# A recurrent kernel on one core: the Vector engine's cube reads a scaled copy of q from SBUF, and two Vector instructions change places

## The reference

```python
def cell(h, x):                                   # layer 0, GRU
    gi = x @ W_ih + b_ih
    gh = h @ W_hh + b_hh                          # 512 x 1536
    r, z = sigmoid(i_r + h_r), sigmoid(i_z + h_z)
    n = tanh(i_n + r * h_n)
    return (1.0 - z) * n + z * h

def derivative(q, p, drive):                      # layer 1, four times per step (Runge-Kutta)
    i_couple = tanh(q) @ coupling.T               # 512 x 512
    dq = q - q ** 3 / 3.0 - p + drive + i_couple + bias
    dp = EPSILON * (q + ALPHA - BETA * p)
    return dq, dp

x = x + scan(cell, cond, x)
x = x + scan(rk4 of derivative, cond, x)          # DT = 0.01, clip to +-20 after each step
```

## Time and profile before

| | before |
|---|---|
| median of 3 runs | 3523.38 us (3521.14 to 3523.52) |
| profiled execution | 3529.05 us, its span 3527.2 us |
| busy: PE / PE weight loads / DVE / ACT / POOL | 98% / 90% / 80% / 74% / 42% |
| granted TensorE clock, mean | 0.987 |

### The profile page before, as it was taken

How to read it: one execution, slowest core, us unless ns; L and a number is a source line. 1 busy time by engine, 2 the same in 40 slices (tenths; PEclk the granted TensorE clock), 3 DMA queues, 4 the chain that set the end, 5 groups by cost and what they waited for, 6 DMA issues and landing times.

```text
span 3527.2 us, 296053 instructions
## 1 busy us (share of the span) xinstructions
PE 3439.5 (98%) x115469; PEld 3178.9 (90%) x115469; DVE 2816.7 (80%) x20699; ACT 2605.1 (74%) x23713; POOL 1478.5 (42%) x6169
## 2 busy tenths in 40 slices
PE   8989999999999999999999999999999999999978
PEld 4479999999999999999999999999999999999954
DVE  2068888888888888888888888888888888888876
ACT  3257777777777777777777777777777777777752
POOL 0024444444444444444444444444444444444421
PEclk9999999999999999999999999999999999999978
DMA  3000000000000000000000000000000000000001
GB/s 131 24 26 1 1 1 1 1 1 1 1 1 1 1 1 1 1 1 1 1 1 1 1 1 1 1 1 1 1 1 1 1 1 1 1 1 1 1 2 48
DMA packets 9433, 24.29 MB, mean 7 GB/s; under 512 B 556, under 2 KB 600, under 8 KB 8792
## 3 DMA queue, kind: packets, MB, share of 16 engines
q1 hardware_dynamic: 8832, 19.92, 1.6%
q10 hardware_dynamic: 88, 0.02, 0.0%
HBM read 15.75 MB, written 4.19 MB: 6 GB/s over the span
## 4 chain that ended last, share of the span: by engine, by line
PE 85%; DVE 7%; ACT 6%; issue 2%; DMA 0%; ACTq 0%; DVEq 0%; POOL 0%; POOLq 0%
PE psum L1187 46%; PE psum L1144 32%; PE psum L1114 5%; ACT tpart L583 2%; PE psum L1290 1%; ACT tfull L585 1%; DVE psum L895 1%; DVE tpart L852 1%; ACT qterm L558 1%; ACT pterm L554 1%; DVE psum L875 1%; DVE qnext L895 1%; DVE psum L887 0%; ACT qterm L547 0%; DVE wih L981 0%
## 5 line engine op out<-in xcount | busy, mean ns | idle before, releaser
L1187 PE MATMUL psum<-tpart,cpl 128*128 128x32 f16 (+1 forms) x65536 | 1966.8, 176 | 21.1 <-DVE tpart L852 14.5
L1187 PEld LDWEIGHTS psum<-tpart,cpl 128*128 128x128 f16 x65536 | 1781.8, 96 | 113.0 <-DVE tpart L852 22.8
L1144 PE MATMUL psum<-hpart,whh 128*128 128x32 f16 x49152 | 1553.3, 177 | 15.9 <-DVE hpart L828 12.0
L1144 PEld LDWEIGHTS psum<-hpart,whh 128*128 128x128 f16 x49152 | 1374.4, 96 | 38.3 <-DVE hpart L828 14.2
L852 DVE TENSOR_TENSOR tpart<-tfull,tpart 128x8 f16<-128x8 f32 x4096 | 682.1, 167 | 154.0 <-ACT tfull L585 11.4
L895 DVE TENSOR_REDUCE psum<-psum 128x8 f32<-128x24 f32 x3072 | 574.8, 188 | 110.1 <-PE psum L1187 3.7
L583 ACT ACTIVATE tpart<-psum 128x8 f16<-128x8 f32 x3072 | 527.3, 172 | 90.5 <-DVE psum L895 18.4
L585 ACT ACTIVATE tfull<-psum 128x8 f32<-128x8 f32 x3072 | 526.4, 172 | 0.0
L583 ACT ACTIVATE tpart<-qnext 128x8 f16<-128x8 f32 x1024 | 213.5, 208 | 312.4 <-DVE qnext L895 312.4
L505 ACT ACTIVATE rz<-gates 128x16 f32<-128x16 f32 x1024 | 241.1, 235 | 267.5 <-DVE gates L787 267.0
L547 ACT ACTIVATE qterm<-psum 128x16 f32<-128x16 f32 x3072 | 413.6, 202 | 0.0
(11 more groups left out here) (153 smaller groups left out, 4449.8 us busy)
## 6 DMA issues: line engine op xcount, KB each, us to landing
xrow<-in_x_dram SPq DMA_DIRECT2D x4, 1024.0 KB, 11.7
out_dram<-space SPq DMA_DIRECT2D x16, 256.0 KB, 2.0
wih<-in_L_cond_W_ih_dram SPq DMA_DIRECT2D x3, 1024.0 KB, 10.2
space<-in_L_cond_W_hh_dram SPq DMA_DIRECT2D x1, 3072.0 KB, 19.1
space<-in_L_cond_coupling_dram SPq DMA_DIRECT2D x1, 1024.0 KB, 19.3
xrow<-in_cond_dram SPq DMA_DIRECT2D x1, 1024.0 KB, 4.7
wih<-in_L_cond_Wk_dram SPq DMA_DIRECT2D x1, 1024.0 KB, 5.7
wih<-in_L_cond_Wo_dram SPq DMA_DIRECT2D x1, 1024.0 KB, 7.9
```

The lines of the kernel that those rows point to most:

```text
L1144: mm = pe.matmul(gate_out[x][:, :, :, c * B:(c + 1) * B], whh[:, w, k, n * P:(n + 1) * P], copies_in(hpart[:, k, :, :]), start=(c == 0 and ...
L1187: mm = pe.matmul(stage_out[a][:, 0:reps, :, col:col + B], cpl[:, w, k, n * P:(n + 1) * P], copies_in(tpart[:, s % 2, k, :, :])[:, 0:reps, ...
```

## The change

Three edits, all in the step that the engines repeat:

1. ScalarE makes one scaled copy of `qt` (`COPY_OF` says which), then the square, and then the other copies. Before, all copies stood ahead of the square. In stages 1 to 3 `cubic` multiplies by that copy in SBUF in place of `qt` in PSUM, and `base` divides its factor out. As the square no longer tells that the copies are made, `sum_stage(s, 0)` of stages 1 and 2, which overwrites `qt`, waits for `qterm_ready[s]` as well. In `cubic(0)` the wait for `q1_ready` is left out (`linear` ahead of it has the same).
2. In stage 2 `sum_gates(1, gru)` stands between `cubic(2)` and `base(2)` in place of behind `base(2)`.
3. In stage 3 `sum_stage(3, 0)` stands ahead of `new_h_full(1, gru)`.

```diff
+COPY_OF = [2, 3, 3]
...
-            def stage_terms(s):
+            def stage_terms(s, rs):
-                for r in range(s + 1, 4):
+                for r in rs:
                     ins = act.activation(in_halves(qterm[:, s + 1, r, :]), qt, ACT.Copy, scale=STEP[s] * sums_of[r][s + 2])
-                ins.then_inc(qterm_ready[s + 1], 1)
+                    if r == s + 1:
+                        ins.then_inc(qterm_ready[s + 1], 1)
...
                     if s < 3:
-                        stage_terms(s)
+                        stage_terms(s, [COPY_OF[s]])
...
                         act.activation(in_halves(sq[:, s_next, :]), arg, ACT.Square,
                                        scale=k_stage[s]).then_inc(sq_ready[s_next], 1)
+                    if s < 2:
+                        stage_terms(s, [r for r in range(3, s, -1) if r != COPY_OF[s]])
...
                     dve.wait_ge(sq_ready[0], v - 1)
-                    dve.wait_ge(q1_ready, v)
...
                     dve.wait_ge(sq_ready[s], v)
-                    dve.scalar_tensor_tensor(in_halves(cub), in_halves(sq[:, s, :]), LINEAR[s], qt,
+                    dve.scalar_tensor_tensor(cub, sq[:, s, :], LINEAR[s], qterm[:, s, COPY_OF[s - 1], :],
                                              ALU.add, ALU.mult).then_inc(cub_ready, 1)
...
-                    dve.scalar_tensor_tensor(stage_base, in_halves(cub), -STEP[s - 1] / 3, in_halves(sums[:, s - 1, :]),
+                    dve.scalar_tensor_tensor(stage_base, in_halves(cub), -1 / (3 * sums_of[COPY_OF[s - 1]][s + 1]),
+                                             in_halves(sums[:, s - 1, :]),
                                              ALU.mult, ALU.add).then_inc(base_ready, 1)
...
                 if a == 0:
                     dve.wait_ge(base_ready, stage_count(s, v))
+                    if s in (1, 2):
+                        dve.wait_ge(qterm_ready[s], v)
...
                 cubic(2, now)
-                base(2, now)
                 if gated_step:
                     sum_gates(1, gru)
+                base(2, now)
...
                     new_high(1, gru)
+                sum_stage(3, 0, now)
+                if gated_step:
                     new_h_full(1, gru)
-
-                sum_stage(3, 0, now)
```

More of the change, by code:

```diff
@@ L874, in cubic @@
                     dve.wait_ge(sq_ready[s], v)
-                    dve.scalar_tensor_tensor(in_halves(cub), in_halves(sq[:, s, :]), LINEAR[s], qt,
+                    dve.scalar_tensor_tensor(cub, sq[:, s, :], LINEAR[s], qterm[:, s, COPY_OF[s - 1], :],
                                              ALU.add, ALU.mult).then_inc(cub_ready, 1)
+            sums_of = recovery_sums()
             def base(s, v):
```

## The result

The changed kernel takes 3500.01 us, the median of 4 runs (3494.10 to 3502.56), beside 3523.38 before: a ratio of 0.9933, with a 95% interval from 0.9921 to 0.9944. That is 23 us less, where 66 were forecast. The profiled execution took 3494.10 us, with a span of 3492.3 and a clock of 0.990 (0.987 before).

A forecast was written before the change was run, and what follows sets the result against it. TensorE bounds the kernel, with some 0.6 us of gaps between groups a step to win. Edits 1, 2 and 3 give 0.11 + 0.08 - 0.06 = 0.13 us a step, times 510 = 66 us: 3457 us, range 3420 to 3500.

The forecast's parts named there:

- rival (b): Stages 1 and 2: later base eats edit 2, third semaphore costs 0.06 us; 0.03 a step, 3508 us; chance 0.12.
- 0.06 a step, between 0 and 0.10: Stage 3: edit 3 gains nothing, delays `h_low` and stops TensorE in group 7; costs 0.06 us a step.
- in the steps with the loop's branch all 0.10 pass on: Ahead of group 0, branch steps: edit 3's whole 0.10 us stop in group 7 delays group 0.
- some 0.03: Ahead of group 0, steps without the branch: of edit 3's 0.10 us stop only some 0.03 passes on.
- Edits 1 and 2 together, 0.19: Groups 4 to 6: edit 1 gives 0.11 us a step and edit 2 0.08.
- group 4 starts 0.11 earlier: Stage 1: edit 1 lets the row sum start at 1596.65, not 1596.76, and group 4 start 0.11 us earlier.
- from it to group 4 the chain is untouched: Stage 1: from row sum to group 4 (tanh twice, low part) nothing changes, so the 0.11 us arrives whole.
- Edit 2, "0.08": Stage 2: gates ahead of base let group 6 start at 1599.01, not 1599.09: 0.08 us, between 0 and 0.21.
- I let it move by 0.06: Cube of stage 2 in VectorE's queue: with edit 1 it comes 0.06 us earlier, bounds 0 and 0.11.
- The third semaphore, 0.02: Row sum's extra wait: costs between 0 and 0.06 us, taken as 0.02.
- Rival (c): Stage 3: cube from SBUF waits for GpSimd's L418, starting 0.19 us later; 15 us slower, 3539 us; chance 0.07.
- Square before copies, and cube from SBUF: Edit 1: copies behind the square cost ScalarE nothing; cube's SBUF input costed at 0, though the skill gives 0.065 us shorter.

The follow-up runs named there:

- e1: The changed kernel without edit 3 (edits 1 and 2 alone): 3440.18 us, ratio 0.9764 to the kernel before.
- e2: The kernel before with edit 3 alone: 3589.44 us, ratio 1.0187 to the kernel before.
- e10: e1 with `h_low` of half 1 behind the second row sum of stage 3: 3534.49 us, ratio 1.0018 to the kernel before.
- e9: The changed kernel with TensorE's loop branch behind group 5 in place of group 7, still two steps a turn: 3461.27 us, ratio 0.9812 to the kernel before.
- e3: The kernel before with edit 1 alone: 3517.21 us, ratio 0.9984 to the kernel before.
- e4: The kernel before with edit 2 alone: 3459.72 us, ratio 0.9822 to the kernel before.
- e12: e3 (edit 1 alone) with GpSimd's `next_x1` ahead of its sum of stage 1: 3493.77 us, ratio 0.9902 to the kernel before.
- e5: e1 with GpSimd's `next_x1` ahead of its sum of stage 1: 3428.08 us, ratio 0.9717 to the kernel before.
- e11: e1 with `next_x1` first, the cube of stage 3 on PSUM and the branch behind group 5: 3425.19 us, ratio 0.9706 to the kernel before.

## Why the prediction was off, point by point

The direction and the places were right. The forecast was 66 us, 23 came. The 43 us between are two terms. That 3500 lies near the 3508 of rival (b) is chance: nothing of what (b) supposes was seen.

- **Edit 3, "0.06 a step, between 0 and 0.10": 0.117 to 0.13** (e1 and e2). This is 29 us of the 43, and the size lay outside the bounds. The mechanism was right to 0.02: the row sum gained nothing, `h_low` came 0.19 later, the hole was 0.12 against 0.10. The step that failed is "in the steps with the loop's branch all 0.10 pass on". There 0.18 passes on, since the gap at the branch grows from 0.15 to 0.21 as well (e1, e10). In the others "some 0.03" was too low: 0.06 in the means, as group 0 has a hole of 0.04 besides. The prediction took the gap ahead of group 0 for a cushion and never asked whether the branch itself depends on what stands ahead of it. It does, by the sequencer's lead (e10), and behind group 5 the branch costs nothing (e9). What the sequencer does in the 0.35 us of a branch isn't shown.
- **Edits 1 and 2 together, 0.19: 0.163** (e1, 83 us), 14 us of the 43. **Edit 1, "group 4 starts 0.11 earlier"**: it starts 0.12 earlier in the means, but has a hole of 0.04, so 0.08 is left. The step that failed is "from it to group 4 the chain is untouched", which holds for half 0 only: on half 1 `argument` was held by GpSimd, the second row sum came late, and the 13th product with it. **Edit 2, "0.08"**: with edit 1 in place the gaps ahead of groups 5 and 6 fall from 0.239 to 0.159 together, 0.08 as forecast. Taken alone the edits give other shares, 0.011 (e3) and 0.123 (e4), and that is no second error: by the prediction's own working edit 1 moves `h_low`, and so group 5, by only 0.06, and edit 2 without edit 1 gives up to 0.13. Measured, edit 1 gives 0.068 once `argument` isn't held (e12), and "I let it move by 0.06" was nearly 0 with the hold. With `next_x1` first edits 1 and 2 give 100 us, 0.195 a step (e5), about the 0.19 forecast; since `weigh` and `h_low` are held there, that match is in part luck.
- **The third semaphore, 0.02**: nothing in either stage. Rival (b) falls.
- **Rival (c), the cube blocked by GpSimd**: it is held, by 0.05 and not 0.16. I dismissed the hold with the row of L821 inside L420, which starts 0.12 behind GpSimd's instruction. The held ones start from 0.05 before it to 0.12 behind it: `argument` in the changed kernel, the cube, `weigh` in e5, the low part in e5 and e11. In all these traces they end 0.02 to 0.04 behind the end of GpSimd's instruction. So how much one loses depends on how much earlier it would have ended: low parts of e5 that start 0.10 to 0.12 behind the sum take 0.19, those from 0.14 on their usual 0.17, and `argument` of before, 0.10 behind, would have ended behind the sum anyway. L821 is of another kind: it ends well inside L420 and is free in all 391 such meetings. L420 is another operation (TENSOR_SCALAR) than the held ones met (TENSOR_TENSOR). The evidence was of the wrong kind, and the instruction that mattered was another than the rival named.
- **Square before copies, and cube from SBUF**: free cubes take 176 to 180 ns with both inputs in SBUF, as before with one in PSUM (177). The 0.065 us that the Trainium skill's figures (VectorE: DVE Perf Modes, section on the TRN2 errata) would give doesn't appear.

What stays open: that e5 and e11 end near the same time, although e11 has one more hold removed and the branch moved, is read from their traces (the held low parts, the gap ahead of group 4); no run takes GpSimd's sum away from all of VectorE's instructions at once, so what the holds cost in all isn't known. Why L420 holds nothing isn't tested either. Cubes of stages 1 and 2 from PSUM with ScalarE's copies behind the square weren't tried.

## What to carry to other kernels

An instruction moved between a producer and its consumer in an in-order queue is paid where the consumer gates another engine; look up that engine's need to the hundredth before calling the gap behind it a cushion, and see whether a loop branch stands there. A branch wants a place in the loop ahead of which nothing waits late, and behind which TensorE has to wait anyway: moving it was worth 43 us here for no work at all. When an edit brings one engine forward against another, list which of its instructions will now start together with the other engine's; the swap of two lines in e4 gave 63 us, and the larger edit 1 ran into a neighbour. The change is best taken without its third edit (e1), with `next_x1` first (e5): 3428 us in place of 3500.

## What was not expected of the hardware

- A GpSimd TENSOR_TENSOR beside a VectorE instruction with two SBUF inputs held VectorE up by up to 0.14 us: the held instruction ended 0.02 to 0.04 us behind GpSimd's. Which of the two gave way was decided within some 0.02 us: `h_low` starting within 0.02 of the 128x32 sum took its usual 0.155 (381 times in the changed kernel, the sum 0.273 in place of 0.251), and starting 0.02 to 0.04 behind it, it took 0.25 (e5). `argument` was held even when it started 0.02 to 0.05 before the sum. What decides there stays open.
- TensorE's loop branch took 0.35 us from its start in the sequencer to the next load. Of it 0.13 to 0.15 us showed as a gap without a wait in the 12 products ahead of it, 0.21 us with one, whether the wait took 0.12 or 0.21, and nothing behind group 5.
- A loop of 4 x 224 products had its instructions loaded again and again (236 packets in place of 17), with 18 stops of 4.8 to 5.3 us in 2500 us; one of 2 x 224 did not.
